# VectorE takes maxima pieces between the dependent steps of its short chains

## What is computed

```python
x = x + attention(layernorm(x), ctx)        # Q = xWq, K = cWk, V = cWv, softmax(QK/4)V, Wo, bo
def fp4_quant_dequant(x):                   # blocks of 16 on the last dimension
    scale = max(|block|) / 6, at least 1e-12
    q = nearest of (0, .5, 1, 1.5, 2, 3, 4, 6) to |block| / scale, times sign, times scale
fp4_linear(x, w) = q(x) @ q(w).T
h = silu(fp4_linear(x1, w_gate)) * fp4_linear(x1, w_up)
out = x1 + fp4_linear(h, w_down)            # x1 = layernorm(x) inside the branch
```

## Time and profile before

| | us |
|---|---|
| median of 3 runs | 3528.58 |
| lowest and highest run | 3525.02, 3530.06 |
| the profiled execution | 3532.97 |
| its span, first to last instruction | 3531.2 |

### The profile page before, as it was taken

One profiled execution on the slowest core, in us unless ns is written; L12 is line 12 of the kernel. 1 busy time (PEld: TensorE's weight loads), 2 busy tenths in 40 slices (PEclk: granted clock), 3 DMA queues, 4 the chain that ended last, 5 costly groups with the idle time before them and its releaser, 6 DMA issues.

```text
span 3531.2 us, 55990 instructions
## 1 busy us (share of the span) xinstructions
PE 3420.3 (97%) x19606; PEld 1560.4 (44%) x19606; DVE 2947.5 (83%) x6697; ACT 2298.8 (65%) x4512; POOL 1036.9 (29%) x1114
## 2 busy tenths in 40 slices
PE   7899999999999999999999999999999999999996
PEld 3333444444444444444444444444444444444334
DVE  6878888888888988888888888988888888888865
ACT  2667666667666667666667666667666667666662
POOL 1323222333322333222333322333222333322222
PEclk7999999999999999999999999999999999999998
DMA  4332233232232332233232232332232232232210
GB/s 81 57 51 45 39 57 50 34 62 36 49 51 44 53 44 45 40 57 48 36 62 35 49 52 43 54 44 43 42 57 46 38 62 32 49 55 35 38 24 8
DMA packets 154263, 163.02 MB, mean 46 GB/s; under 512 B 58071, under 2 KB 127080, under 8 KB 153984
## 3 DMA queue, kind: packets, MB, share of 16 engines
q1 hardware_dynamic: 153984, 159.45, 28.6%
HBM read 46.22 MB, written 8.39 MB: 15 GB/s over the span
## 4 chain that ended last, share of the span: by engine, by line
PE 72%; DVE 23%; ACT 2%; POOL 1%; issue 1%; DMA 1%; SPq 1%; ACTq 0%; DVEq 0%
PE out_ps L912 18%; PE score_ps L901 16%; PE piece_ps L926 16%; DVE piece_max L1264 13%; PE work L865 6%; PE work L876 4%; PE work L840 3%; PE work L832 3%; ACT probs L1028 1%; PE work L856 1%; PE work L821 1%; DVE ctx_T L1134 1%; DVE ctx_T L1130 1%; PE work L850 1%; PE work L873 1%
## 5 line engine op out<-in xcount | busy, mean ns | idle before, releaser
L1028 ACT ACTIVATE probs<-score_ps 128x512 f32<-128x512 f32 (+1 forms) x3328 | 1884.0, 600 | 923.7 <-PE score_ps L901 916.0
L1264 DVE TENSOR_REDUCE piece_max<-piece_ps 128x1 f32<-128x400 f32 (+1 forms) x4096 | 2110.3, 566 | 360.6 <-PE piece_ps L926 347.8
L926 PE MATMUL piece_ps<-k_stack,q_stack 96*128 96x400 bf16 (+1 forms) x4096 | 1297.5, 339 | 40.2 <-DVE piece_max L1264 28.2
L901 PE MATMUL score_ps<-q_stack,k_stack 99*128 99x512 bf16 (+1 forms) x3328 | 1252.2, 385 | 19.6 <-DMA q_stack<-neg_rows 5.3
L912 PE MATMUL out_ps<-probs,v_ones 128*17 128x512 f32 x6656 | 877.1, 599 | 0.4
L926 PEld LDWEIGHTS piece_ps<-k_stack,q_stack 96*128 96x128 bf16 x4096 | 386.0, 98 | 801.9 <-DVE piece_max L1264 548.2
L901 PEld LDWEIGHTS score_ps<-q_stack,k_stack 99*128 99x128 bf16 (+1 forms) x3328 | 324.2, 99 | 641.7 <-ACT probs L1028 494.4
L1316 POOL TENSOR_TENSOR h<-h,h_grid 128x704 f32<-128x704 f32 (+1 forms) x68 | 111.8, 1644 | 888.4 <-DVE h_grid L1092 888.4
L865 PE MATMUL work<-wgu_T,xq_T 128*128 128x512 f32 (+1 forms) x1080 | 333.7, 425 | 0.5
L912 PEld LDWEIGHTS out_ps<-probs,v_ones 128*17 128x17 f32 x6656 | 110.3, 95 | 269.4 <-issue 218.4
L865 PEld LDWEIGHTS work<-wgu_T,xq_T 128*128 128x128 f32 x1080 | 198.1, 191 | 43.9 <-issue 3.8
(11 more groups left out here) (173 smaller groups left out, 2893.4 us busy)
## 6 DMA issues: line engine op xcount, KB each, us to landing
k_stack<-k_parts SPq DMA_DIRECT2D x256, 150.1 KB, 3.6
k_stack<-k_parts SPq DMA_DIRECT2D x256, 100.1 KB, 3.9
ctx_in<-in_ctx SPq DMA_DIRECT2D x47, 384.0 KB, 3.8
k_stack<-k_parts SPq DMA_DIRECT2D x256, 50.0 KB, 3.7
q_stack<-q_parts SPq DMA_DIRECT2D x256, 48.0 KB, 2.8
x_in<-in_x SPq DMA_DIRECT2D x16, 512.0 KB, 5.0
q_stack<-q_parts SPq DMA_DIRECT2D x256, 32.0 KB, 2.1
resid<-in_x SPq DMA_DIRECT2D x62, 128.0 KB, 2.6
```

The source lines that it names most:

```text
L901: pe.matmul(score_ps[0:r, n % SCORE_RING, :], k_stack[:, par, slot(g, j), m * P:m * P + r], q_stack[:, par, slot(g, j), :], start=True, st ...
L926: pe.matmul(piece_ps[:, n % PIECE_RING, 0:hi - lo], q_stack[0:SROWS, par, slot(g, j), t * P:(t + 1) * P], k_stack[0:SROWS, par, slot(g, j) ...
L1028: act.activation(probs[0:r, step % 2, j, :], score_ps[0:r, (PER_GROUP * m + j) % SCORE_RING, :], ACT.Exp, scale=SCORE_SCALE).then_inc(prob ...
L1264: dve.tensor_reduce(piece_max[:, row, c:c + 1], piece_ps[:, n % PIECE_RING, 0:piece_at[c + 1] - piece_at[c]], AX_X, ALU.max).then_inc(piec ...
```

## The change

`fp4_small`, `fp4_grid`, and the chains of `heads_out` and `gate_up` become generators. Each gives up control (`yield`) ahead of every step that waits for the result of the step before; `handle` is a generator too. The loop runs the first part of a chain at its old place, then one part behind each piece. When the next event or drain is due, or the list ends, what is left of the chain runs at once (`finish`). So p pieces behind an event separate at most p steps. No operation is added, removed or changed, and the lists of the other engines stay as they are. `h_small` and `h_grid` have a `yield` in front of their first step too, so they begin one piece later.

```diff
             def fp4_small(small, done, base):
                 amax, scale, inv = (small[:, i, :] for i in range(3))
+                yield
                 dve.wait_ge(done, base(1))
                 dve.tensor_scalar(scale, amax, 1.0 / 6.0, TINY, ALU.mult, ALU.max).then_inc(done, 1)
+                yield
                 dve.wait_ge(done, base(2))
                 dve.reciprocal(amax, scale).then_inc(done, 1)
+                yield
                 dve.wait_ge(done, base(3))
                 dve.tensor_scalar(inv, amax, BELOW_TIE, None, ALU.mult).then_inc(done, 1)
...
             def fp4_grid(src, grid, done, base):
+                yield
                 dve.wait_ge(done, base(5))
                 dve.tensor_scalar(grid.bitcast(I32), src.bitcast(I32), EXPONENT_BITS, None, ALU.bitwise_and).then_inc(done, 1)
+                yield
                 dve.wait_ge(done, base(6))
                 dve.tensor_scalar(grid, grid, 1.0, ROUNDER, ALU.max, ALU.mult).then_inc(done, 1)
...
                     dve.reciprocal(inv_sum[:], v[:, :, :, HEAD_DIM]).then_inc(inv_ready, 1)
+                    yield
                     dve.wait_ge(inv_ready, count(of, PHASES, g + 1))
...
+                    yield
                     dve.wait_ge(silu_step, count(old, n * QT, n * t + j + 1))
...
+            def finish(steps):
+                for _ in steps:
+                    pass
...
             def body(kind, batch):
-                drain = None
+                drain, rest = None, iter(())
                 for what, *item in SEQUENCE[kind]:
                     if what == "piece":
                         reduce_piece(next_groups_batch(kind, batch, item[0]), *item)
+                        next(rest, None)
                     if drain and (what == "piece" or  what == "event" and item[0][0] not in ROUNDS
                                   or what == "round" and item[1] == 0):
-                        handle(kind, batch, drain)
+                        finish(rest)
+                        rest = handle(kind, batch, drain)
+                        next(rest, None)
                         drain = None
                     if what == "event" and item[0][0] not in ROUNDS:
-                        handle(kind, batch, item[0])
+                        finish(rest)
+                        rest = handle(kind, batch, item[0])
+                        next(rest, None)
                     elif what == "round" and item[1] == len(round_parts(item[0])) - 1:
                         drain = item[0]
+                finish(rest)
                 if drain:
-                    handle(kind, batch, drain)
+                    finish(handle(kind, batch, drain))
```

More of the change, by code:

```diff
@@ L1206, in handle @@
                     fp4_max(q.xq, q.xq_small, xq_step)
-                    fp4_small(q.xq_small, xq_step, lambda k: count(old, 7 * QT, 7 * t + k))
+                    yield from fp4_small(q.xq_small, xq_step, lambda k: count(old, 7 * QT, 7 * t + k))
                 elif name == "xq_scale":
@@ L1212, in handle @@
                     fp4_scale(q.xq, q.xq_small, xq_step, base)
-                    fp4_grid(q.xq, q.xq_grid, xq_step, base)
+                    yield from fp4_grid(q.xq, q.xq_grid, xq_step, base)
                 elif name == "gate_up":
@@ L1231, in handle @@
                     elif name == "h_small":
-                        fp4_small(q.h_small, h_step, base)
+                        yield from fp4_small(q.h_small, h_step, base)
                     elif name == "h_scale":
@@ L1235, in handle @@
                     else:
-                        fp4_grid(src, q.h_grid, h_step, base)
+                        yield from fp4_grid(src, q.h_grid, h_step, base)
                         if kind == "tail" and t in VECTOR_ROUNDS:
@@ L1249, in handle @@
                         fp4_max(src, small, w_step)
-                        fp4_small(small, w_step, base)
+                        yield from fp4_small(small, w_step, base)
                     elif name == "w_scale":
@@ L1253, in handle @@
                     else:
-                        fp4_grid(src, h_grid[0:src.shape[0], 0:src.shape[1]], w_step, base)
+                        yield from fp4_grid(src, h_grid[0:src.shape[0], 0:src.shape[1]], w_step, base)
                 elif name == "down":
```

## The result

| | before | changed |
|---|---|---|
| median | 3527.69 us (5 runs) | 3553.46 us (5 runs) |
| lowest and highest | 3525.02, 3530.06 | 3545.83, 3567.39 |
| the profiled execution | 3532.97 us | 3567.39 us |
| span of it, granted clock | 3531.2 us, 0.988 | 3565.6 us, 0.983 |

The changed kernel is slower by the factor 1.0081, with a 95% interval of 1.0052 to 1.0110: 26 us. The forecast was 3539, some 11 us slower, and a range up to 3554. The sign was right, the size was less than half. The changed kernel also scatters over 22 us, the kernel before over 5. Its two longest runs, 3567.4 and 3564.9, have a mean granted clock of 0.983, the other three (3553.5, 3547.9, 3545.8) 0.988 to 0.989.

A forecast was written before the change was run, and what follows sets the result against it. PE was taken to bound the kernel. Losses of 1.71 less gains of 0.63 us in 14 middle sequences (+15.1), -4 for the first and -0.5 for the last gave +10.6 us: 3539 us, range 3516 to 3554.

The forecast's parts named there:

- What bounds the kernel: PE bounds it; DVE costs PE no more than 2 to 3 us per middle sequence.
- The price of an edge: A dependent DVE edge costs 0.118 us more; 481 edges make 57 us of DVE's time, nearly all off the path.
- xq_scale/1: Two PE stalls for pieces go, one moves to the third piece: net gain 0.26 us per middle sequence.
- h_small/1: A PE piece 0.50 us late comes earlier as three edges before it go: gain 0.27 us per middle sequence.
- h_grid/3: Its second step waits behind a piece, delaying POOL and PE's transpose: loss 0.83 us per middle sequence.
- gate_up/2/1: Its chain ends 0.38 us later and PE's next round on the bank waits: loss 0.19 us per middle sequence.
- gate_up/0/2: It waits for a piece that isn't there, delaying max_parts/1 and pieces behind: loss 0.14 us per middle sequence.
- gate_up/1/0: A loss like that of gate_up/2/1, of 0.04 us per middle sequence.
- h_small/2: Steps wait behind a late piece, so h_scale/2 and the next piece come later: net loss 0.44 us per middle sequence.
- First and last sequence: First: 36 edges gain 4 us where PE waits for DVE. Last: -0.5 us, gains against an xq_T without slack.
- The clearly slower one: Rival: waits for absent pieces make a backlog that hits the ring each time, 2.6 us per sequence: 3556; chance 0.06.
- The one in which edges are worth nothing: Rival: separated steps cost DVE as much as chained ones, only losses stay, 24 us: 3553; chance 0.02.

The follow-up runs named there:

- only_gate_up: The kernel before, with the chains of gate_up alone in steps (163 edges): 3530.7 us, ratio 1.0008.
- only_small2: The kernel before, with the event h_small/2 alone run in steps: 3550.0 us, ratio 1.0062.
- pool_waits2: The changed kernel, with POOL's split of k_proj/0/2 also waiting until h_scale/2 is done, DVE's order unchanged: 3542.7 us, ratio 1.0032.
- grid3_whole: The changed kernel, with h_grid/3 running both its steps at once: 3541.9 us, ratio 1.0035.
- probe1440: The kernel before, with an unused DVE reduction over 1440 columns ahead of h_scale/2 in the middle sequences: 3589.3 us, ratio 1.0179.
- probe720: The kernel before, with an unused DVE reduction over 720 columns ahead of h_scale/2 in the middle sequences: 3544.8 us, ratio 1.0053.
- small2_whole: The changed kernel, with h_small/2 running its three steps at once as before: 3526.1 us, ratio 0.9997.

## Why the prediction was right or wrong

- **What bounds the kernel**: right. DVE's share of the chain fell by ten points, its wait for pieces grew from 348 to 418 us, and the kernel got no faster. `only_gate_up` shows it in pure form.
- **The price of an edge**, 0.118 us: right, by the rows of `gate_up` above. Their worth on the path, nearly nothing: right.
- **Gains**: `xq_scale/1` 0.26 forecast; PE's stalls there fell from 0.73 to 0.49 us, 0.24. `h_small/1` 0.27 forecast, 0.34 measured. Missed: 0.3 us at `ln2_apply/1` (0.49 us of stalls), a collision with POOL that is gone, where I had 0.07 us of loss.
- **Losses**: `h_grid/3` 0.83 forecast, 0.87 us measured ahead of L873. `gate_up/2/1` 0.19 forecast, 0.21 measured, in the changed kernel as in `only_gate_up`. Over-sized were `gate_up/0/2` (0.14: the transpose is some 0.1 us late, of which 0.02 to 0.05 stay) and `gate_up/1/0` (0.04, none seen).
- **The step that failed: `h_small/2`.** The mechanism was right, the step waits for a piece that isn't there and what is behind it comes 0.46 us late. The term was 0.44 us; `only_small2` measured 1.2 us in the sequences in which the clock didn't fall. I took `h_scale/2` to last its 0.88 us of before. Moved by half a microsecond it met a POOL operation that had begun 0.18 us earlier and was held for the rest of it. `pool_waits2` takes that away, and with it the term is right: against the kernel before an earlier stall of 0.18 us is gone, one of 0.54 has come, and 0.09 follow, 0.45 net. (The working shows only 0.30 us and a signal of it; the rest of the 0.44 isn't written out.) That its middle sequences are then 1.0 us longer than before and my sum said 1.08 is chance: the vanished collision and the run's own stall of 0.4 us, neither in the sum, nearly cancel.
- **What was not in the sum at all: the clock.** I had worked out stalls only by their own length. Each fall behind this stall cost 1.6 to 1.7 us, and the profiled execution had fourteen, 24 us. That this is also why runs of one binary lie 22 us apart is an estimate: fourteen falls of 3.4 us at half the clock lower its mean by 0.007, and the slowest runs have 0.983 where the fastest has 0.989. Only one of them has a trace.
- **First and last sequence**: -4 and -0.5 forecast, neither shown. The first took 3.0 us less, but unchanged code scatters there by 2.7 us.
- **The rivals**: two had the right size and the wrong price list. The clearly slower one gave 3556; its backlog at the ring was one place, not each. The one in which edges are worth nothing gave 3553, the measured median, but the rows of `gate_up` show the edge gone, and the places of its losses aren't those that cost. So the time alone would have picked a wrong cause.
- **The range**: its upper end of 3554 is called that of the doubled losses, but 14 x (3.42 - 0.63) - 4.5 gives 3563; 3554 is the forecast's net effect doubled. That the median lies inside is luck.

In numbers, per middle sequence: forecast +1.08; measured +3.1 in the profiled execution. About 0.8 of that is the collision at `h_small/2`, 1.6 the clock, -0.3 the collision that vanished, and the rest, 1.0, is what I had summed.

## What to carry to other kernels

Filling the gaps between dependent operations of an engine that isn't the bound gave nothing by itself here. What counts is where the bounding engine waits for it, and a step put behind other work inherits that work's wait: read for each place whether the filler is there yet. A schedule tuned by hand or by search is worth changing place by place; the same edit in all places hid a gain of 0.5% behind a loss of 1.3%.

## What the hardware showed that I hadn't expected

- Some operations of VectorE and GpSimd hold each other, and who starts first wins: a 704-column product took 0.88 or 1.74 us, a 256-column `tensor_scalar` 0.41 or 0.94 to 0.96 us, decided by 0.15 to 0.6 us of lead. The pieces, reductions out of PSUM, aren't held: in the changed kernel six took 2.97 us as ever while two GpSimd operations of 1.67 us ran. The Trainium skill's page "SBUF — State Buffer", section "SBUF: two separate sides", describes an exclusive lock for the length of an instruction that the first to start gets, for VectorE operations with two SBUF inputs or in a two-port mode. The product has two such inputs and agrees; in which mode the `tensor_scalar` ran no trace here shows.
- TensorE's clock fell from 2.4 to 1.2 GHz for some 3.4 us behind idles of 1.23 us (in 14 of 14 middle sequences of the changed kernel's profiled execution, in 7 of 14 of `grid3_whole` and of `only_small2`), and for 3.4 or 6.8 us behind idles of 2.15 us (14 of 14 of `probe1440`). It didn't behind idles of 1.04 us (`probe720`) and 0.71 us (`small2_whole`). Each fall of 3.4 us cost 1.6 to 1.7 us. The same idle in the same place did or didn't bring it down, in `grid3_whole` in turns.
